# First feed-forward of a two-layer decoder: every expert over every token, or chosen rows scattered into pages by expert

## The chip, the cores and the metric

The kernel runs on one core of one Trainium2 chip, in float32. TensorE does the matmuls (PE; its weight loads are PEld), VectorE is DVE, ScalarE is ACT, GpSimd is POOL, and SyncE (SP) issues DMAs. An engine followed by q (SPq) is that engine's instruction queue. The metric is the device time in microseconds (us).

## The reference

4096 tokens (4 sequences of 1024) of width 256 pass two layers, each with a self attention, a cross attention to 77 context rows, and a feed-forward, all with a residual sum and a layer norm behind them. The change is in the feed-forward of the first layer:

```python
probs = jax.nn.softmax(xf @ router_w + router_b, axis=-1)       # 64 experts
tw, ti = jax.lax.top_k(probs, 8)
tw = tw / jnp.sum(tw, axis=-1, keepdims=True)
def body(acc, p):                                                # one expert, 256 -> 64 -> 256
    W1, B1, W2, B2, e = p
    h = jax.nn.silu(xf @ W1 + B1) @ W2 + B2
    cw = jnp.sum(jnp.where(ti == e, tw, 0.0), axis=-1)           # 0 where e is not chosen
    return (acc + cw[:, None] * h, None)
shared = jnp.sum(jax.vmap(shared_mlp)(sw1, sb1, sw2, sb2), axis=0)   # 2 experts, 256 -> 512 -> 256, all tokens
```

Each token has 8 of 64 experts with a weight other than zero; the reference computes all 64 for all tokens. The router, the choice, the shared experts and the sum over b2 weighted by `cw` belong to it too.

## The kernel before

`decoder` (L1553) runs five phases, one after another, with a barrier and a clearing of semaphores between them (`end_phase`, L1576): attention of layer 0, feed-forward of layer 0, attention of layer 1, feed-forward of layer 1, and the last sum.

**Attention of layer 0** (`attention_phase`, L116) walks the sequence in 8 steps of 128 positions, 4 sequences at once. An order written by hand, `SEQUENCE0` (L91), is the same for every engine: each entry is a stage, how many steps it lags behind, and a part. Iteration n runs a stage with lag a for step n - a; there are 8 iterations plus the largest lag (2). The parts that matter here:

- `ln1` (lag 0, last in the sequence) and `ln2` (lag 2): POOL makes the scale of a layer norm (`norm_scale`, L376: four small operations, L379 to L382), ACT applies it (L486, L496), and POOL adds a bias for the residual (`x1b` L403, `x2s` L411). `x1t`, the first stage of the next iteration, has PE transpose what `ln1` made (L848).
- `wout` (lag 1): PE projects the attention (L965), DVE adds the residual and takes the sums of the norm (L520 to L526), on which POOL's next L379 waits. Its last part stands between `pv` part 3 (DVE: reciprocal and product, L659, L660) and `ln1`.
- `rt`, `top`, `cwt`, `b2` (lag 2): router logits, their softmax and the eight largest (DVE L667 to L688), the weights `cw` transposed and stored to DRAM as `cw1`, and the product with b2 summed into `x2s`, which goes to DRAM as `res1`.
- `ret`, `mx` and `sc` share one PSUM area of four banks ("wide"); the others turn over four banks.

Every engine keeps its instructions in order, so an operation that is late holds back all behind it on that engine. SP prefetches both expert weights, `w1` and `w2` (4096 KB each, L1589 and L1590), into the halves of the tile `big` during this phase.

**Feed-forward of layer 0** (`shared_routed_phase`, L998) goes over 8 tiles of 512 tokens. Each tile has 40 units: 8 of 128 hidden columns of the shared experts, and 32 pairs of routed experts (2 x 64 hidden columns). For each unit PE makes the hidden rows (`hidden`: 2 matmuls over 512 columns), ACT applies bias and silu (L1124), DVE multiplies a routed unit by the token weights of its two experts (L1135, `cw` loaded by broadcasting DMAs, L1063), and PE sums the unit into four output banks (`outward`: 4 matmuls over 256 columns). A float32 matmul appears as two matmul instructions. The tile ends with the residual and a layer norm.

**Attention of layer 1** scatters token rows by expert with indirect DMAs issued by POOL (L423), 8 for each step, 128 rows each, and its feed-forward (`gated_phase`, L1205) reads them back in tiles of 128 rows, transposes them on PE (L1417, L1438), and scatters results (L1309).

## Time and profile before

| | us |
|---|---|
| median of 3 runs (2778.97 to 2783.06) | 2782.24 |
| profiled execution | 2779.99 |
| its span, first to last instruction | 2778.3 |
| attention of layer 0, from 0 to | 532 |
| feed-forward of layer 0, 532 to 1664 | 1132 |
| attention of layer 1, 1664 to 2207 | 543 |
| feed-forward of layer 1, 2207 to 2711 | 504 |
| last sum, 2711 to 2778 | 67 |

Over the span PE is busy 86%, DVE 32%, ACT 23%, POOL 11%; the granted clock of TensorE is 0.92 of full on average. The `windows` view gives, for each stretch, its length, then for PE, PEld, DVE, ACT and POOL the busy time and, in brackets, the number of instructions, and last the granted clock (1.00 is 2.4 GHz, 0.50 is 1.2 GHz), the busy share of the 16 DMA engines and the GB/s that they moved. A line of the timeline gives start and duration in us, engine, source line, operation, what is written and read, and the count of merged instructions; in square brackets stands how long the engine was idle before it, and for whom it waited. A merged line's duration runs to the modelled end of its last instruction; the start of the next line tells better when PE was free.

### The profile page before, as it was taken

What the parts mean: (1) busy time and instruction counts of PE and PEld (TensorE: products, weight loads), DVE (VectorE), ACT (ScalarE), POOL (GpSimd) and SP (SyncE); (2) the same over time, 40 slices, a digit from 0 to 9 for tenths busy, and PEclk for the clock granted to TensorE, in tenths of its full rate; (3) what the DMA queues carried; (4) which work ended last, traced back from release to release, by engine and by line L of the source; (5) the groups of instructions that cost most, each with busy time, mean ns of one, the idle gap of its engine ahead of it and who ended that gap; (6) DMA issues with size and microseconds to landing.
All of it is one profiled execution on the core that took longest, in us unless ns stands there. A gap on an engine that the chain in (4) does not pass through costs nothing. (4 is left out here: it accounts for less than half of the span.)

```text
span 2778.3 us, 47409 instructions
## 1 busy us (share of the span) xinstructions
PE 2379.0 (86%) x18834; PEld 1644.7 (59%) x18835; DVE 895.1 (32%) x2013; ACT 651.8 (23%) x972; POOL 299.1 (11%) x428
## 2 busy tenths in 40 slices
PE   5999898599999999999999975788878259999980
PEld 3777667366666666666666653566656235555550
DVE  4556565212121212121212122445553212222216
ACT  1333223112222212122222111333233012222220
POOL 0111111000000000000000000122321201111111
PEclk9999998699999999999999996789887579999995
DMA  6011100423232323232333224011100321111117
GB/s 200 25 35 37 57 27 27 114 50 77 68 84 61 84 61 84 61 84 63 81 65 80 53 53 168 17 33 38 49 32 25 104 84 42 42 44 44 42 36 242
DMA packets 136392, 185.35 MB, mean 67 GB/s; under 512 B 14379, under 2 KB 94495, under 8 KB 135327
## 3 DMA queue, kind: packets, MB, share of 16 engines
q1 hardware_dynamic: 124319, 156.43, 21.0%
q0 software_dynamic: 7680, 22.16, 2.2%
q10 hardware_dynamic: 4224, 4.19, 0.5%
q8 instruction: 143, 2.34, 0.4%
q14 instruction: 26, 0.21, 0.0%
HBM read 140.65 MB, written 42.11 MB: 66 GB/s over the span
## 5 line engine op out<-in xcount | busy, mean ns | idle before, releaser
L1189 PE MATMUL b_yp<-big,b_h 128*128 128x256 f32 x2048 | 481.2, 379 | 0.0
L1177 PE MATMUL b_hp<-b_xt,big 128*128 128x512 f32 x1024 | 481.2, 592 | 0.0
L1189 PEld LDWEIGHTS b_yp<-big,b_h 128*128 128x128 f32 x2048 | 389.1, 190 | 155.3 <-issue 114.8
L1135 DVE TENSOR_TENSOR b_h<-b_h,b_cw 128x512 f32<-128x512 f32 x256 | 177.3, 693 | 873.9 <-ACT b_h L1124 873.9
L1124 ACT ACTIVATE b_h<-b_hp,b_b 128x512 f32<-128x512 f32 x256 | 176.0, 687 | 705.5 <-PE b_hp L1177 705.5
L1177 PEld LDWEIGHTS b_hp<-b_xt,big 128*128 128x128 f32 x1024 | 194.6, 190 | 135.7 <-issue 122.5
L473 ACT ACTIVATE pt<-wide 77x2048 f32<-77x2048 f32 x64 | 119.9, 1874 | 146.3 <-PE wide L945 146.3
L1429 PE MATMUL d_gp<-big,d_xt 128*128 x288 | 143.9, 622 | 9.8 <-issue 0.6
L1342 DVE TENSOR_TENSOR d_h<-d_gate,d_up 128x512 f32<-128x512 f32 x72 | 49.5, 688 | 298.2 <-PE d_up L1429 298.2
L659 DVE RECIPROCAL rden<-bank 128x256 f32<-128x256 f32 x64 | 112.2, 1754 | 98.2 <-PE bank L957 97.7
L1177 PE MATMUL b_hp<-b_xt,b_sw 128*128 128x512 f32 x256 | 119.7, 601 | 20.1 <-DMA b_sb<-in_L_sb 18.9
L1447 PE MATMUL d_yp<-d_wd,d_ht 128*128 x576 | 136.2, 379 | 0.8 <-ACT d_ht L1326 0.8
L1447 PEld LDWEIGHTS d_yp<-d_wd,d_ht 128*128 128x128 f32 x576 | 109.4, 190 | 46.1 <-issue 35.0
L1429 PE MATMUL d_up<-big,d_xt 128*128 x288 | 135.3, 592 | 0.0
L1189 PEld LDWEIGHTS b_yp<-b_sw,b_h 128*128 128x128 f32 x512 | 97.3, 190 | 40.5 <-issue 30.6
L1189 PE MATMUL b_yp<-b_sw,b_h 128*128 128x256 f32 x512 | 121.0, 379 | 0.0
L1103 POOL TENSOR_TENSOR b_mv<-b_mv,b_eps 128x4 f32<-128x4 f32 x8 | 1.6, 195 | 1092.9 <-DVE b_mv L1156 1092.9
L945 PE MATMUL wide<-peak_t,sel 32*77 32x128 f32 x2048 | 112.6, 289 | 0.1
L652 DVE TENSOR_REDUCE peak<-wide 128x16 f32<-128x1232 f32 x64 | 92.0, 1437 | 33.6 <-PE wide L929 31.4
L965 PE MATMUL bank<-wout,att_t 128*128 128x256 f32 x256 | 74.6, 442 | 28.7 <-DVE att_t L660 28.7
L1429 PEld LDWEIGHTS d_up<-big,d_xt 128*128 128x128 f32 x288 | 54.8, 190 | 69.2 <-issue 69.2
L777 PE MATMUL bank<-xt,wqk 128*128 128x512 f32 x128 | 65.6, 641 | 26.6 <-DVE ones L577 26.6
(237 smaller groups left out, 2817.5 us busy)
## 6 DMA issues: line engine op xcount, KB each, us to landing
b_cw<-cw SPq DMA_DIRECT2D x128, 512.0 KB, 7.5
d_x<-lists SPq DMA_DIRECT2D x72, 130.0 KB
big<-in_L_w SPq DMA_DIRECT2D x2, 4096.0 KB, 20.7
f_y<-results SPq DMA_DIRECT2D x16, 512.0 KB, 7.8
x<-in_x SPq DMA_DIRECT2D x8, 512.0 KB
xt<-in_x_t SPq DMA_DIRECT2D x32, 128.0 KB, 3.2
res_t<-x2t SPq DMA_DIRECT2D x32, 128.0 KB, 1.9
res<-x2s SPq DMA_DIRECT2D x8, 512.0 KB, 3.2
```

The lines of the kernel that those rows point to most:

```text
L473: empties(nc.scalar.activation(pt[0:CTX, p % 2].rearrange("k (j n) -> k j n", j=4), ps[0:CTX], ACT.Exp, scale=score_scale), job)
L652: empties(nc.vector.tensor_reduce(peak[:, p].rearrange("p (j n) -> p j n", j=4)[:, :, 0:4], ps[:, :, 0:4 * CTX].rearrange("p j (n k) -> p ...
L659: step(nc.vector.reciprocal(rden[:, p % 2], ps[:, KC * P:]))
L777: ins = mm(out[:], wqk[:, c, p * P:(p + 1) * P], xt[:, i % 2, c], start=c == 0, stop=c == KC - 1)
L945: ins = mm(out[0:CTX, r, n * P:(n + 1) * P], sel[quarter(r), n], peak_t[quarter(r), toks(p)], start=False, stop=True, skip_group_check=True)
L965: ins = mm(out[:, bb * DM:(bb + 1) * DM], att_t[:, c, toks(2 * p + bb)], wout[:, c], start=c == 0, stop=c == KC - 1)
L1124: nc.scalar.activation(h[:, u % 4], hp[u % 4][:], ACT.Silu, bias=bias).then_inc(h_done, 1)
L1135: nc.vector.tensor_tensor(h[:, u % 4], h[:, u % 4], cw[:, g % 2, p % G], ALU.mult)\
L1177: ins = mm(hp[u % 4][:], w, xt[:, k, c], start=c == 0, stop=c == KC - 1)
L1189: ins = mm(yp[t][:, 0:DM], h[:, u % 4, t * P:(t + 1) * P], sw2[:, u] if u < CH else w2[:, u - CH], start=u == 0, stop=u == UNITS - 1)
L1429: ins = mm(out[k][:], xt[:, k, c], w[:, c, bass.ds(e * H1, H1)], start=c == 0, stop=c == KC - 1)
L1447: ins = mm(yp[:, 0:DM], ht[:, k, c], wd_flat[:, bass.ds(e * (HC * DM) + c * DM, DM)], start=c == 0, stop=c == HC - 1)
```

## The change

Layer 0's feed-forward becomes two phases, and its attention phase gets the work that sorts rows by expert.

1. **Attention of layer 0.** `cw1` and its store go. Two stages without matmuls are new, `put` and `weigh`, both with lag 3, so there is an eleventh iteration; `rank` (lag 2) stands after `b2` and before `pv` part 3. DRAM tensors `lists0` and `results0` have 192 pages of 256 rows of 1 KB, 50.3 MB each. ACT fills `lists0` with zeros ahead of the scatters: ten DMAs of 2 MB at `v` of step 0, two at `v` of each later step. `top` gives the chosen mask and counts as well. `rank` is three float32 matmuls on PE (positions before each token, by a triangular matrix, and totals) and some 20 operations on DVE that turn them into a page and a row for each of a token's 8 choices, kept in the SBUF tile `slots0`. `put` has POOL issue 32 indirect DMAs for each step (4 sequences x 8 choices), each storing 128 rows of 1 KB. `weigh` is three DVE operations over 2048 elements that leave the eight weights in `weights0`. The tile `z2` gets three buffers, so that `wout` waits for the scatters of three steps ago.
2. **`expert_phase`.** `w2` is loaded here, all 64 experts into both halves of the partitions (two DMAs of 4096 KB), no longer in the attention phase. From the page ends DVE works out the expert of each page. Then 96 pairs of pages follow: two loads of 256 KB on SP, 8 transposes (PE), the chosen expert's weights copied by DVE to a small tile at an address that it reads as a value from SBUF, hidden rows and outputs on PE in two halves of the array, moves by ACT and DVE, and two stores of 256 KB issued by POOL.
3. **`combine_phase`.** The 8 tiles of 512 tokens keep only the 8 shared units. POOL gathers each tile's 4 x 8 x 128 rows by 32 indirect DMAs, two tiles ahead of the sums; DVE adds them, weighted, to the tile in 32 operations, and the layer norm follows.

The core of the diff:

```diff
-    ("v", 0, 0), ("ln2", 2, 0), ("x2t", 2, 0), ("x2t", 2, 1),
-    ("ret", 0, 0), ("mt", 1, 0), ("v", 0, 1), ("kt", 0, 0),
+    ("v", 0, 0), ("ln2", 2, 0), ("put", 3, 0), ("x2t", 2, 0), ("x2t", 2, 1),
+    ("ret", 0, 0), ("mt", 1, 0), ("v", 0, 1), ("kt", 0, 0), ("weigh", 3, 0),
...
+    ("rank", 2, 0),
     ("pv", 1, 3), ("wout", 1, 1), ("ln1", 0, 0),
...
+                if stage == "put":
+                    pool.wait_ge(slot_done, i + 1)
+                    pool.wait_ge(blank[i], 16 * len(blanks(i)))
+                    for b in range(NB):
+                        for k in range(K0):
+                            pool.indirect_dma_start(
+                                out=lists, out_offset=bass.IndirectOffsetOnAxis(ap=slots[:, b, i, k:k + 1], axis=0),
+                                in_=z2[i % 3][:, b, :], in_offset=None).then_inc(scattered[i % 3], 16)
...
+                if stage == "v" and p == 0:
+                    act.wait_ge(pool_ready, 3)
+                    for n in blanks(i):
+                        act.dma_start(lists[n * 8 * R0:(n + 1) * 8 * R0, :].rearrange("(p t) n -> p t n", p=P),
+                                      zero[:].unsqueeze(1).broadcast_to([P, 8 * R0 // P, DM])).then_inc(blank[i], 16)
...
+                if stage == "weigh":
+                    dve.wait_ge(cw_done, i + 1)
+                    step(nc.vector.tensor_tensor(same, place[:].unsqueeze(2).broadcast_to([P, NB, K0, E]),
+                                                 slot[:].unsqueeze(3).broadcast_to([P, NB, K0, E]), ALU.is_equal))
+                    step(nc.vector.tensor_tensor(same, same, cw[:].unsqueeze(2).broadcast_to([P, NB, K0, E]), ALU.mult))
+                    step(nc.vector.tensor_reduce(weights[:, :, i, :], same, AX.X, ALU.add))
...
+def expert_phase(nc, sems, d, w1, w_in, lists, page_ends, results):
...
+        @block.sync
+        def _(sp):
...
+            for j in range(PAIRS):
+                if j >= NX:
+                    for h in range(2):
+                        sp.wait_ge(x_full[h], j - NX + 1)
+                for h in range(2):
+                    sp.dma_start(x[:, j % NX, h], rows_of(lists, 2 * j + h)).then_inc(x_in[j % NX], 16)
...
+        @block.gpsimd
+        def _(pool):
...
+                    pool.wait_ge(y_done[h], j + 1)
+                    pool.dma_start(rows_of(results, 2 * j + h), y[:, j % NY, h]).then_inc(sent[j % NY], 16)
...
+        @block.scalar
+        def _(act):
...
+                    turn_out(move, act, 1, j + 1)
+                act.wait_ge(h_full, j + 1)
+                act.wait_ge(staged, 4 * (j + 1))
+                nc.scalar.activation(ht[:, j % 2], hp[j % 2][:, 0:R0], ACT.Silu, bias=w2s[:, j % NW, DM:DM + 1])\
+                    .then_inc(h_done, 1)
+                if j:
+                    rows_out(j - 1)
...
+            def stage(j):
...
+                for h in range(2):
+                    lanes = slice(h * H0, (h + 1) * H0)
+                    e = dve.value_load(plan_i[0:1, j, h:h + 1], min_val=0, max_val=E0 - 1)
+                    nc.vector.tensor_copy(w1s[:, j % NW, h], w1[:, :, bass.ds(e * H0, H0)]).then_inc(staged, 1)
+                    nc.vector.tensor_copy(w2s[lanes, j % NW],
+                                          w2[lanes].rearrange("p e n -> p (e n)")[:, bass.ds(e * (DM + 1), DM + 1)])\
+                        .then_inc(staged, 1)
...
+            def inward(j):
...
+                for c in range(KC):
+                    for h in range(2):
+                        ins = mm(hp[j % 2][h * H0:(h + 1) * H0, 0:R0], w1s[:, j % NW, h, c], xt[:, j % 2, h, c],
+                                 start=c == 0, stop=c == KC - 1)
...
+            def outward(j):
...
+                for t in range(2):
+                    for h in range(2):
+                        ins = mm(yp[h][:, t * DM:(t + 1) * DM], ht[lanes, j % 2, t * P:(t + 1) * P],
+                                 w2s[lanes, j % NW, 0:DM], start=True, stop=True)
...
+            for j in range(PAIRS):
+                if j + 1 < PAIRS:
+                    rows_in(j + 1)
+                inward(j)
+                if j:
+                    outward(j - 1)
...
+def combine_phase(nc, sems, d, src, src_t, results, slots, weights, dst):
...
+            def pick(T):
+                if T >= 2:
+                    pool.wait_ge(summed, (T - 1) * (K0 + 1))
+                for k in range(K0):
+                    for t in range(SUB):
+                        b, i = T // 2, (T % 2) * SUB + t
+                        pool.indirect_dma_start(
+                            out=picked[:, T % 2, t, k, :], out_offset=None, in_=results,
+                            in_offset=bass.IndirectOffsetOnAxis(ap=slots[:, b, i, k:k + 1], axis=0))\
+                            .then_inc(got[T % 2], 16)
...
+                for n in range(K0):
+                    for t in range(SUB):
+                        b, i = T // 2, (T % 2) * SUB + t
+                        ins = nc.vector.scalar_tensor_tensor(out=acc[:, t], in0=picked[:, k, t, n],
+                                                             scalar=weights[:, b, i, n:n + 1], in1=acc[:, t],
+                                                             op0=ALU.mult, op1=ALU.add)
+                    ins.then_inc(summed, 1)
```

## Rows read from the trace of the kernel before

**Rows 1.** The `windows` view by stage: start:end, then busy time and count by engine.

```profile
532.00:1664.00 1132.00, 1104.58 (x3840) 729.91 (x3840) 213.94 (x392) 230.31 (x329) 16.50 (x29) 0.99 0.31 73
...
1969.00:2026.00 57.00, 46.48 (x718) 36.54 (x718) 29.72 (x84) 19.08 (x28) 15.20 (x18) 0.85 0.12 39
```

**Rows 2.** Groups of instructions by line: busy us, mean ns of one.

```profile
L1189 PE MATMUL b_yp<-big,b_h 128*128 128x256 f32 x2048 | 481.2, 379 | 0.0
L1177 PE MATMUL b_hp<-b_xt,big 128*128 128x512 f32 x1024 | 481.2, 592 | 0.0
...
L432 ACT ACTIVATE x1t<-bank 128x512 f32<-128x512 f32 x32 | 18.7, 597 | 93.2 <-PE bank L848 92.4
...
L686 DVE SCALAR_TENSOR_TENSOR rest<-rest,ex 128x256 f32<-128x256 f32 x8 | 3.4, 425 | 0.3
```

**Rows 3.** Timeline of layer 0 attention, one step, then its end: start us, us.

```profile
331.94 0.20 POOL L379 TENSOR_TENSOR rs<-mv,eps 128x4 f32<-128x4 f32 x1 [27.50 <-DVE mv L526]
...
343.16 1.83 PE L848 MATMUL bank<-ident,x 128*128 128x128 f32 x8
...
359.99 2.36 POOL L411 TENSOR_TENSOR x2s<-z,sb 128x1024 f32<-128x1024 f32 x1 [11.62 <-ACT z L496]
...
389.63 0.20 POOL L379 TENSOR_TENSOR rs<-mv,eps 128x4 f32<-128x4 f32 x1 [27.28 <-DVE mv L526]
...
458.65 1.92 PE L848 MATMUL bank<-ident,x 128*128 128x128 f32 x8
...
507.36 0.20 POOL L379 TENSOR_TENSOR rs<-mv,eps 128x4 f32<-128x4 f32 x1 [38.97 <-DVE mv L526]
...
528.15 0.38 SPq L355 DMA_DIRECT2D res<-x2s  x1
```

**Rows 4.** Timeline of POOL, layer 1: first and last of eight indirect DMAs.

```profile
1887.04 1.06 POOL L423 DMA_INDIRECT lists<-rows,slot_u  x1 [25.36 <-DVE slot_u L719]
...
1896.01 0.96 POOL L423 DMA_INDIRECT lists<-rows,slot_u  x1 [0.30 <-issue]
```

**Rows 5.** Timeline of DVE and PE in the step of rows 3.

```profile
340.47 2.89 PE L965 MATMUL bank<-wout,att_t 128*128 128x256 f32 x8 [2.43 <-DVE att_t L660]
...
361.86 2.29 DVE L588 TENSOR_TENSOR prob<-wide,causal 128x2048 f32<-128x2048 f32 x1 [4.95 <-PE wide L800]
...
368.42 0.42 DVE L667 TENSOR_TENSOR lg<-bank,router_b 128x256 f32<-128x256 f32 x1 [4.28 <-PE bank L973]
```

**Rows 6.** Timeline of PE: matmuls on parts of the array, and transposes.

```profile
2010.67 0.66 PE L890 MATMUL bank<-v,tri 128*128 128x65 f32 x4
...
2011.26 0.49 PE L887 MATMUL bank<-state,sig 64*128 64x130 f32 x4
...
2020.06 2.08 PE L911 MATMUL bank<-wo,combt 64*128 64x256 f32 x8
...
2033.19 1.95 PE L857 MATMUL bank<-xt,wlin 128*64 128x256 f32 x16
...
2262.64 0.60 PE L1438 MATMUL d_hp<-d_ident,d_h 128*128 128x128 f32 x4
```

**Rows 7.** The `windows` view: stretches with much DMA, and the one of 2020.06.

```profile
20.00:40.00 20.00, 13.40 (x63) 7.58 (x64) 9.81 (x27) 0.60 (x1) 0.00 (x0) 1.00 1.04 380
...
2020.10:2022.00 1.90, 1.90 (x12) 1.14 (x8) 1.44 (x1) 0.00 (x0) 0.00 (x0) 0.50 0.00 0
...
2720.00:2735.00 15.00, 0.00 (x0) 0.00 (x0) 11.88 (x29) 0.00 (x0) 2.45 (x4) 0.50 0.92 288
...
2735.00:2778.00 43.00, 0.00 (x0) 0.00 (x0) 30.86 (x83) 0.00 (x0) 7.28 (x12) 0.50 0.68 224
```

**Rows 8.** Timeline of SP: issues of DMAs.

```profile
16.16 0.80 SPq L1590 DMA_DIRECT2D big<-in_L_w  x1
...
2236.04 8.01 SPq L1285 DMA_DIRECT2D lists<-d_padding  x8
```

**Rows 9.** Section 6 of the page: KB each, us from issue to landing.

```profile
results<-d_y,d_dest POOLq DMA_INDIRECT x72, 2.4
```

More of the change, by code:

```diff
@@ L27 @@
 CAP = NT + P
+K0 = 8
+R0 = 2 * P
+PAIRS0 = (NT * K0 // R0 + E0) // 2
+ROWS0 = 2 * PAIRS0 * R0
 ROWS1 = NT * K1 // P + E1
@@ L73 @@
 WIDE = ("ret", "mx", "sc")
-MARKS = ("ln1", "ln2", "top")
+MARKS = ("ln1", "ln2", "top", "put", "weigh")
 def steady(sequence):
@@ L190, in attention_phase @@
             kr = sb("kr", [P, NB, DM])
-            prob = sb("prob", [P, 2, 4 * 4 * P])
+            prob = spare[:, 0:4096].rearrange("p (h n) -> p h n", h=2)
+            same = spare[:, 4096:6144].rearrange("p (b k e) -> p b k e", b=NB, k=K0)
+            z2 += [spare[:, n:n + 1024].rearrange("p (b n) -> p b n", b=NB) for n in (6144, 7168)]
+            before = sb("before", [P, P])
+            ones_sq = sb("ones_sq", [P, P])
+            ones_row = sb("ones_row", [P, E])
+            zero = sb("zero", [P, DM])
+            pages_i = sb("pages_i", [P, 2, 2, E], mybir.dt.int32)
+            pages = sb("pages", [P, 2, E])
+            base = sb("base", [P, E])
+            book = sb("book", [P, 4, E])
+            late = sb("late", [P, NB, E])
+            chosen = sb("chosen", [P, NB, E])
+            counts = sb("counts", [P, NB + 1, E])
+            place = sb("place", [P, NB, E])
+            slot = sb("slot", [P, NB, K0])
             ctx_rows = prob[0:CTX, 0, 0:NB * DM].rearrange("k (b n) -> k b n", b=NB)
@@ L259, in attention_phase @@
         sent_rows = sem("sent_rows")
+        mask_done = sem("mask_done")
+        slot_done = sem("slot_done")
+        scattered = [sem(f"scattered{k}") for k in range(3 if first else 1)]
         if first:
@@ L263, in attention_phase @@
             sent_cols = sem("sent_cols")
-            sent_cw = sem("sent_cw")
+            blank = [sem(f"blank{i}") for i in range(STEPS)]
         else:
@@ L388, in _ @@
             nc.gpsimd.memset(peak[:], 0.0).then_inc(pool_ready, 1)
+            if first:
+                nc.gpsimd.memset(zero[:], 0.0).then_inc(pool_ready, 1)
             if not first:
@@ L416, in _ @@
                             .then_inc(copy_done, 1)
-                if stage == "rank":
+                if stage == "put":
[6 more added lines that the diff above has]
+                                in_=z2[i % 3][:, b, :], in_offset=None).then_inc(scattered[i % 3], 16)
+                if stage == "rank" and not first:
                     pool.wait_ge(slot_done, i + 1)
@@ L845, in _ @@
                         b = 2 * p + bb
-                        of = x[:, i % 2, b] if stage != "x2t" else z2[:, b] if first else rows[:, b, 0, 0:DM]
+                        of = x[:, i % 2, b] if stage != "x2t" else z2[i % 3][:, b] if first else rows[:, b, 0, 0:DM]
                         for c in range(KC):
@@ L1085, in _ @@
-            load(0, slice(0, TOK))
+            load(0)
             for a, b in loads:
                 sp.dma_start(a, b).then_inc(consts, 16)
-            weights(0, slice(0, TOK), range(2), first=True)
-            load(1, slice(TOK, 2 * TOK))
-            weights(0, slice(0, TOK), range(2, GROUPS), first=True)
-            with sp.Fori(0, TILES // 2 - 1) as i:
-                for k in range(2):
-                    tile(2 * i + k + 1, k)
-            weights(TILES - 1, slice((TILES - 1) * TOK, TILES * TOK), range(GROUPS))
+            load(1)
@@ L1096, in _ @@
+            for T in range(TILES):
+                sp.wait_ge(out_done, T + 1)
+                sp.dma_start(dst[T * TOK:(T + 1) * TOK, :].rearrange("(t p) n -> p t n", p=P), out[:, T % 2])\
+                    .then_inc(sent[T % 2], 16)
+                if T + 2 < TILES:
+                    sp.wait_ge(y_full, T + 1)
+                    load(T + 2)
+            for k in range(2):
+                sp.wait_ge(sent[k], 16 * TILES // 2)
         @block.gpsimd
         def _(pool):
-            nc.gpsimd.memset(half[:], -0.5)
```

477 lines of the change are left out of this document (313 added, 164 removed).

## The prediction

> **What bounds the kernel now.** I read the `windows` view by stage first. The feed-forward of layer 0 takes 1132 us and PE is busy 1104.6 of them at a granted clock of 0.99 [rows 1]: nothing but TensorE ends there. It does 8 x 40 = 320 units, so a unit costs 1104.6 / 320 = 3.45 us. Four fifths of them (256) are routed pairs, 32 for each tile; DVE and ACT, busy 214 and 230 us, hide behind them. In the groups by line the reader sees that half of this goes into the outward and half into the inward matmuls, 481.2 us each for the routed pairs [rows 2].
>
> Then I read the timeline of the attention step, since the change adds work to all of its engines. A step is 389.63 - 331.94 = 57.7 us from one `ln1` on POOL to the next [rows 3]. PE sets it, except at the end: there PE waits 2.43 us for DVE's last `att_t` [rows 5], so what DVE gets ahead of that product lengthens the step one for one. POOL is nearly idle: its last operation in the step is `x2s` at 359.99, and nothing follows until 389.63 [rows 3].
>
> **The change part by part.** The sum is made against the profiled execution, 2779.99 us (span 2778.3 and 1.7 around it), 2.3 us under the median of the runs.
>
> *Attention, the steps.* `rank` puts about 20 dependent operations on DVE just ahead of `pv` part 3. No row has them. By the neighbours, those over 256 elements take 0.42 us [rows 5] and the small ones about 0.2 (four values take POOL 0.20 [rows 3]): 5 x 0.45 + 12 x 0.25 + four maxima 0.6 + two copies 0.4 = 6.2 us, nearly all on the path. `top` gets one more operation over 256 elements and four short additions, 1.4 us, in a stretch in which DVE has no gap. `weigh` is three operations over 2048 elements of 2.29 us [rows 5], 7 us; between the causal product at 361.86 and the logits at 368.42 DVE idles 4.28 [rows 5], so 2.7 come out late and, wide being held longer, about 1 reaches PE. That makes 8.5 us a step; I take 7.5 for step 2, which has no `weigh`, and 8.5 for five more: 50 us. Bounds: 6 us a step from what follows, and 14 if all of DVE's work counts.
>
> POOL's own cycle must fit too. Consecutive indirect DMAs start (1896.01 - 1887.04) / 7 = 1.28 us apart [rows 4], so 32 take 41.0. From the transposes of `x1t` (343.16) to `x2s` (359.99) are 16.8 us [rows 3]; then 2.4 for `x2s`, 41.0 for `put`, 1.8 for the scale and 2.1 for ACT's norm: 64.2 us, against 57.7 + 8.5 = 66.2 by DVE. So `put` hides behind `rank`; were `rank` free, `put` would still make the step 6.4 us longer. Behind `put` on POOL stands `ln1`, and for it waits the whole next step.
>
> *Attention, the end.* Nothing hides the last scatters. Before, the stage ends 532.0 - 458.65 = 73.4 us after the last `x1t` transposes, and the last `ln2` scale starts 507.36 - 458.65 = 48.7 after them [rows 3]. After: 48.7 + 8.5, then 6.2 for scale, norm and `x2s`, then `put` of steps 6 and 7 one after the other, 82.0, landing 2.4 [rows 9] and barrier 1.4: 149.2. That adds 76 us. With 2 us for two more loads and the memsets at the start, attention costs 2 + 50 + 76 = **+128 us**.
>
> The zero fills are 50.3 MB on ACT's queue, ten of 2 MB at once in step 0. An issue of 4096 KB in 1 KB pieces took SP 0.80 us [rows 8]; ACT idles at `v`, so I cost them at nothing. The trace shows no queue that deep. If ACT had to wait for the queue, up to 21 MB / 288 GB/s [rows 7] = 73 us would be added, once.
>
> *Pages.* PE per pair: 8 transposes at 0.11 us (four take 0.60 with their tail [rows 6]) = 0.9. Inward: 8 instructions of 256 columns in two column halves; 16 such take 1.95 us [rows 6], 8 take 0.94. Outward: 8 instructions in two row halves; 8 took 2.08 us, but at a granted clock of 0.50 [rows 6, 7], so 1.0 at full clock: the halves overlap. Each pair switches the array's form three times. Four 65-column matmuls between two other forms occupy 2011.26 - 2010.67 = 0.59 us where their columns need 0.22 [rows 6]; I take 0.2 per switch. PE: 0.9 + 0.94 + 1.0 + 0.6 = 3.4 us.
>
> The Trainium skill states this switch as a rule, in "TensorEngine Tiling (Array Packing)", Key Properties: changing the tiling mode drains the array. It gives no figure; with no drain the pair would cost PE 2.8 us and the phase 58 us less.
>
> ACT per pair: three moves of 512 columns at 0.60 [rows 2] and a silu of 256, about 0.4 by the same row, 2.2 us. DVE: 0.6 for the turn, four copies of 128 to 257 columns, about 1.1, and two values read into registers. SP's eight issues with such a read took 8.01 us [rows 8], so a read is under 1.0 and DVE under 3.7, in parallel. DMA: 96 pairs move 100.7 MB, 1.05 MB each. At 380 GB/s (large pieces) that is 2.8 us, at 288 (1 KB pieces) 3.6 [rows 7]; these are 2 KB. Three resources thus lie between 3 and 3.7 us. They don't interlock perfectly, so I take the upper end, 3.7, and 96 x 3.7 = 355 us. Ahead of it w2 must land, 8.4 MB at 288 GB/s, 29 us, and x behind it, 4; the last pair and its store add 6, the barrier 2: 396 us.
>
> *Combination.* PE needs 64 x 3.45 = 221 us and POOL 256 x 1.28 = 328: POOL bounds. Seven layer norm scales between gathers, 1.4 each, add 10, the start 1. After the last gather: landing 2.4, 32 sums on DVE of 0.425 [rows 2] = 13.6 and 0.6 of semaphores, norm 4.6, store 2.4, barrier 2: 25. Together 364 us. Whether a gather costs POOL what a scatter does no row shows; from below the columns of the shared units bound the phase (221 + 35), from above see the rivals.
>
> *Sum.* 396 + 364 = 760 for 1132: -372. With +128: 2780 - 244 = **2536 us**.
>
> **The rivals.**
>
> *A, POOL's descriptor work collides with DVE.* During the gathers DVE runs 256 sums whose two inputs both lie in SBUF. If POOL stood still for each, the phase would gain 256 x 0.425 = 109 us [rows 2]: 2645. Against it: the eight scatters of rows 4 kept their pitch while DVE worked, though not with such sums. The Trainium skill, "SBUF — State Buffer", Who interferes with whom, says that a DVE instruction with two SBUF inputs contends with a GpSimd instruction that reads SBUF, and that two-port copies keep GpSimd from writing descriptors; no run so far shows either here.
>
> *B, the pages are paced by data.* In the last 43 us of the kernel, loads and stores mixed reach 224 GB/s [rows 7], though they don't fill the engines there (0.68). At that rate 100.7 MB take 450 us, 95 more: 2631. Or PE loses its clock while waiting: at 0.50 the pair costs 2 x 2.8 + 0.6 = 6.2 us, 240 us more, 2776. Against this speaks layer 1's attention, where PE is busy 46.5 of 57 us and keeps 0.85 [rows 1].
>
> *C, ACT is stopped by the fills:* 40 to 73 us more, 2576 to 2609.
>
> *D, slower than before: an indirect DMA in a long burst costs more than in one of eight.* 512 of them are added in all. The five hidden bursts have 2 us of slack each, so 512 x (p - 1.28) - 10 reaches 244 at p = 1.78 us. At 2.0 us the price is 359 and the time 2895. For it: no burst here is longer than eight; against it: within eight the pitch does not grow (0.96 and 0.30 idle at the last [rows 4]), and each moves 128 KB in 1.28 us, 102 GB/s, far from 288.
>
> *E, better overlap:* pairs at 3.0 us and `rank` cheaper (6 us a step): 2536 - 67 - 15 = 2454.
>
> **How the numbers follow.** Forecast 0.50, A 0.14, B 0.15 (0.02 of it above 2775), C 0.06, D 0.07, E 0.08. The forecast's own range is 2480 to 2610. The range that should hold the time 8 times in 10 runs from 2452 to 2680: it leaves out D, the clockless B and the lower half of E, and some of A and B together. A measurement of this kernel tells 0.2%, 5.6 us, from no change. Faster: all but D, a part of B and their mixtures, 0.90; within: 0.01; slower: 0.09.
>
> **What would show it.** In the trace after: an eleventh iteration of attention with nothing but 32 DMAs on POOL, twice; steps of 66 us, PE waiting some 8 for DVE's `att_t`; ACT's fills issued without a gap. In the pages a pitch of 3.7 us with PE's clock above 0.9 and neither ACT nor DVE without gaps. In the combination POOL back to back at 1.28 us with PE idle a third of the time; a pitch above 1.5 there is A or D, and A if it grows only while DVE sums. The prediction is wrong if pairs take over 5 us, if a burst of 32 slows as it goes, or if ACT stands in step 0.

## The result, and the profile after

The changed kernel takes 2917.1 us (median of 4 runs, 2908.8 to 2921.9) beside 2780.6 for the kernel before on the same chip: ratio 1.049, interval 1.046 to 1.053. The prediction was 2536, faster; the kernel is slower. The profiled execution took 2921.9 us (span 2920.1). By stage, from the `windows` view (columns as in [rows 1]):

```profile
197.00:300.60 103.60, 70.46 (x963) 48.65 (x962) 48.23 (x94) 18.76 (x25) 40.54 (x41) 0.77 0.31 103
300.60:405.00 104.40, 70.34 (x958) 48.51 (x957) 48.35 (x94) 18.67 (x25) 40.81 (x43) 0.75 0.31 102
...
927.90:1304.80 376.90, 302.58 (x2306) 198.87 (x2306) 162.21 (x490) 198.37 (x385) 103.47 (x193) 0.91 0.91 291
1304.80:1804.10 499.30, 261.66 (x768) 161.64 (x768) 143.93 (x384) 43.14 (x65) 255.50 (x275) 0.72 0.32 97
```

The first two rows are steps of attention with a `put`: 104 us where the prediction had 66, and neither PE (70 us busy) nor POOL (41) fills them. The third is the pages, 377 us (predicted 396). The fourth is the combination, 499 (364). Pages and combination together save 256 us of the 1132 of [rows 1]. But attention ends at 927.9 instead of 532.0, 396 us later (predicted 128). Measured on ACT's `ln1` moves, that is 37 at the start, 234 in the seven steps between the first and the last, and 125 behind the last one.

The timeline of one step shows what stands there. POOL's first and last scatter, then PE and ACT (`issue`: the engine waited for nothing that the profile shows; `remote`: for a signal whose sender it does not name):

```profile
441.47 1.04 POOL L447 DMA_INDIRECT lists<-big,slots  x1 [0.16 <-issue]
...
482.81 0.96 POOL L447 DMA_INDIRECT lists<-big,slots  x1 [0.30 <-issue]
...
449.47 0.40 PE L907 MATMUL bank<-big,v 128*32 128x128 f32 x8
...
474.77 0.37 PE L1047 MATMUL bank<-pt,vals 77*32 77x128 f32 x1 [1.72 <-issue]
475.47 0.37 PE L1047 MATMUL bank<-pt,vals 77*32 77x128 f32 x1 [0.33 <-issue]
477.58 0.37 PE L1047 MATMUL bank<-pt,vals 77*32 77x128 f32 x1 [1.74 <-issue]
...
488.07 0.86 PE L1047 MATMUL bank<-pt,vals 77*32 77x128 f32 x10 [0.33 <-issue]
...
488.17 0.60 ACT L468 ACTIVATE ot<-bank 128x512 f32<-128x512 f32 x1 [35.92 <-remote]
```

POOL does nearly what was forecast: 32 scatters start 1.26 us apart, save for two early gaps of 2.3 us, and the last is no slower than in [rows 4]. PE does not. Some 8 us into this burst its groups of eight matmuls fall apart into single ones, started at multiples of 0.7 us, and the idle time ahead of them is put down to `issue`: PE thins out. At 488.07, 4 us after the burst, ten go out at once. PE's clock follows: 0.75 over such a step, 0.50 late in the burst.

The combination shows the same (groups by line, columns as in [rows 2]; third, the idle time and its causes):

```profile
L1374 POOL DMA_INDIRECT b_picked<-results,slots x256 | 245.5, 959 | 77.6 <-issue 77.0 <-POOL b_eps L1380 0.6
L1456 PE MATMUL b_yp<-b_sw,b_h 128*128 128x256 f32 x512 | 139.8, 428 | 155.9 <-issue 81.6 <-ACT b_h L1399 74.3
L1448 PE MATMUL b_hp<-b_xt,b_sw 128*128 128x512 f32 x256 | 134.2, 640 | 69.1 <-issue 41.7 <-DMA b_sb<-in_L_sb 27.3
L1399 ACT ACTIVATE b_h<-b_hp,b_sb 128x512 f32<-128x512 f32 x64 | 43.1, 687 | 438.3 <-remote 215.3 <-PE b_hp L1448 152.1 <-issue 70.9
L1415 DVE SCALAR_TENSOR_TENSOR b_acc<-b_picked,weights,b_acc 128x256 f32<-128x256 f32 x256 | 107.1, 481 | 2.3
```

A gather costs POOL 0.959 us plus 0.30, so 256 of them take 322 us, as forecast. Yet they don't run in one piece. They come in four runs of 64 with gaps of 34 to 38 us: the gathers of tile T + 2 wait until DVE has summed tile T, which waits for PE, and late in each run PE all but stands still (from 1445 to 1508 it is busy 13 of 63 us). What was to overlap comes one after the other.

The start is a matter of its own (timeline of ACT, after, then before):

```profile
1.62 73.86 ACTq L479 DMA_DIRECT2D lists<-zero  x10
75.51 1.28 ACT L468 ACT_TABLE_LOAD   x1 [75.51 <-issue]
76.81 1.09 ACT L468 ACTIVATE v<-bank 128x512 f32<-128x512 f32 x2
```

```profile
37.52 0.60 ACT L432 ACTIVATE v<-bank 128x512 f32<-128x512 f32 x1 [35.38 <-PE bank L782]
```

Ten fills of 2 MB hold ACT for 73.9 us, so its first move of `v` comes 39 us late. The loads are late as well: PE's first matmul starts at 45.31 in place of 26.60. But PE then waits 16.7 us more for ACT's `v`.

### The profile page after: what moved, and what is told of

It is laid out like the page before. It is cut to its first block and busy times, and to the rows that moved or that the text cites. A ratio compares the mean times of both kernels' runs of the same rounds, so it can differ in the third digit from the quotient of the medians.

```text
span 2920.1 us, 47524 instructions
## 1 busy us (share of the span) xinstructions
PE 1946.5 (67%) x18116; PEld 1324.2 (45%) x18117; DVE 1096.4 (38%) x2738; ACT 662.4 (23%) x1093; POOL 908.5 (31%) x1125
## 5 line engine op out<-in xcount | busy, mean ns | idle before, releaser
L1374 POOL DMA_INDIRECT b_picked<-results,slots x256 | 245.5, 959 | 77.6 <-issue 77.0
L1456 PE MATMUL b_yp<-b_sw,b_h 128*128 128x256 f32 x512 | 139.8, 428 | 155.9 <-issue 81.6
L1169 POOL DMA_DIRECT2D results<-e_y x192 | 103.4, 543 | 271.1 <-ACT e_y L1181 268.5
L1448 PE MATMUL b_hp<-b_xt,b_sw 128*128 128x512 f32 x256 | 134.2, 640 | 69.1 <-issue 41.7
L447 POOL DMA_INDIRECT lists<-big,slots x160 | 162.5, 1016 | 48.2 <-issue 47.9
L1047 PE MATMUL bank<-pt,vals 77*32 77x128 f32 x2048 | 105.4, 286 | 96.5 <-issue 96.4
L1399 ACT ACTIVATE b_h<-b_hp,b_sb 128x512 f32<-128x512 f32 x64 | 43.1, 687 | 438.3 <-remote 215.3
L1265 PE MATMUL e_xp<-e_ident,e_x 128*128 128x128 f32 x768 | 106.4, 283 | 42.7 <-DMA e_x<-lists 42.7
L456 POOL DMA_INDIRECT lists<-rows,slot_u x64 | 62.2, 972 | 211.8 <-DVE slot_u L803 194.8
L1408 DVE TENSOR_TENSOR b_acc<-b_yp,b_xr 128x256 f32<-128x256 f32 x32 | 11.3, 418 | 309.5 <-PE b_yp L1456 286.3
L1047 PEld LDWEIGHTS bank<-pt,vals 77*32 77x32 f32 x2048 | 62.9, 112 | 134.9 <-issue 133.7
```

The costliest lines, as they stand in the source:

```text
L447: pool.indirect_dma_start(out=lists, out_offset=bass.IndirectOffsetOnAxis(ap=slots[:, b, i, k:k + 1], axis=0), in_=z2[i % 3][:, b, :], in_ ...
L1047: ins = mm(out[quarter(r), at:at + P], left, pt[0:CTX, p % 2, of:of + P], start=h == 0, stop=h == 1, skip_group_check=True)
L1169: pool.dma_start(rows_of(results, 2 * j + h), y[:, j % NY, h]).then_inc(sent[j % NY], 16)
L1265: ins = tr(xp[h][j % 2][:, (t * KC + c) * P:(t * KC + c + 1) * P], x[:, j % NX, h, t, c * P:(c + 1) * P], ident[:])
L1374: pool.indirect_dma_start(out=picked[:, T % 2, t, k, :], out_offset=None, in_=results, in_offset=bass.IndirectOffsetOnAxis(ap=slots[:, b, ...
L1448: ins = mm(hp[u % 4][:], sw1[:, c, u * P:(u + 1) * P], xt[:, T % 2, c], start=c == 0, stop=c == KC - 1)
```

## The experiments

Each study ran on one chip with the kernel before beside it: e1 to e4, e5 to e8, e9 to e12, e13 to f2 and the last two runs. The five studies ran on five different chips, which turns out to matter. The changed kernel itself did not run again, but kernels with its unpaced bursts did in the first two studies (e1_loops, e4_latefill, e7_fills_bursts8), and their steps took 104 to 106 us as its own did. My theory after the first look (F): a long burst of indirect DMAs keeps the engines' instructions from being fetched.

**e1_loops.** PE's and ACT's code of the combination in loops:

```
-            for T in range(TILES):
+            with pe.Fori(0, TILES // 2) as i:
+                for k in range(2):
+                    T = 2 * i + k
```

> The combination of layer 0 takes 499 us in the changed kernel (1304.8 to 1804.1), 135 more than predicted; PE's records there thin out to single matmuls with idle time put down to issue, and only while POOL issues its gathers. Here PE's and ACT's instructions of the combination stand in loops (PE two tiles an iteration, ACT one) instead of being written out; every matmul, move, gather and wait is the same. Theory F (instruction supply: during a long burst of POOL's indirect DMAs the instruction streams of the other engines are not refilled, and written-out code runs dry): the loop's code is fetched once, PE no longer thins out, POOL's gathers run back to back, the combination takes 365 to 385 us and the whole 2780 to 2805. Rival T (the transfers of the gathers, or their descriptors, slow PE or its semaphores themselves): the same 499 us, 2917 within 10. In between, 420 to 460 us for the combination, would say that only one of the two engines was short of instructions, or only for a part of the time.

2933.2 us against 2785.3; the combination takes 505 us, no less than the 499 of the changed kernel. The packets of the instruction queue in that stage (queue table: packets, MB, share) fell from 7 to 2, the first row from the changed kernel, the second from this one:

```profile
q8 instruction: 7, 0.11, 0.1%
```

```profile
q8 instruction: 2, 0.03, 0.0%
```

So the loops needed next to no new instruction packets, and PE thinned out all the same. That fells F, as far as it means fetching code from DRAM. The Trainium skill, "Runtime: NRT & Kernel Launch", Instruction fetch mechanics, says that instructions are streamed in blocks of 16 KiB by a queue of their own, mostly hidden. The profile of the changed kernel agrees on the blocks (134 packets, 2.20 MB, so 16.4 KB each).

**e2_noput.** No scatters in attention:

```
-                            pool.indirect_dma_start(
-                                out=lists, ...).then_inc(scattered[i % 3], 16)
```

> Left out of the computation: the 256 scatters of the attention stage (the pages stay zero), with the waits on them; rank, weigh and the slots are computed as before, and the fills, pages and gathers stay. Attention ends at 927.9 us in the changed kernel, its steps 3 to 7 take 104.5 each against 66 predicted. If the scatters are what lengthens the steps (theories F and T alike): steps of 64 to 68 us, attention ends at 532 + 37 (late start) + 50 + 10 = 620 to 640, the whole 2615 to 2640. Rival R (rank and weigh on DVE, with their waits, are what lengthens them): steps stay above 90 us, the end falls only by the two bursts after the last step, 82 us, and the whole is about 2835.

2619.3 us, ratio 0.941 (the pages stay zero, so it leaves out a part of the computation). Steps of 65.3 us, attention ends at 627.5. `rank` and `weigh` cost what was forecast (66.2; PE waits 7.0 us for `att_t`, forecast 8). The scatters alone cost 300 us of attention; on this chip, against e1_loops and e4_latefill, 302 and 312.

**e3_plain.** The same bytes as plain DMAs:

```
-                            pool.indirect_dma_start(
+                            at = ((i * NB + b) * K0 + k) * P
+                            pool.dma_start(lists[at:at + P, :], z2[i % 3][:, b, :])
```

> Each of the 256 scatters of the attention stage is replaced by a plain DMA of the same 128 KB from the same tile to a fixed stretch of the pages, issued by POOL at the same place (which leaves the rows of the pages in another order than the computation needs). Same bytes, same count of instructions on POOL, no indices. Theory F1 (what starves the others is that the descriptors of an indirect DMA are written by software): steps near 66 us, attention ends below 700, the whole 2660 to 2720. Rival B (the bytes or the rows of 1 KB, whoever describes them, take the DMA engines from what the other engines need): steps stay within 10 us of 104 or, as plain DMAs are issued faster, are shorter only by the part of the burst that vanishes, 20 us or so: 84, the whole above 2780.

2636.9 us. From its timeline, 32 plain DMAs and the next `ln1` pair:

```profile
323.33 0.20 POOL L402 TENSOR_TENSOR rs<-mv,eps 128x4 f32<-128x4 f32 x1 [13.44 <-DVE mv L564]
...
359.52 17.12 POOL L448 DMA_DIRECT2D lists<-big  x32
...
389.23 0.20 POOL L402 TENSOR_TENSOR rs<-mv,eps 128x4 f32<-128x4 f32 x1 [12.58 <-DVE mv L564]
```

They go out at 0.53 us each, more than twice the bandwidth of the scatters, and the step is 65.9 us. They use the same queue as the scatters (`q0 software_dynamic`, 1536 packets and 4.20 MB between 359 and 389 us), so it is not the queue either. What slows PE is the indirect kind, not the traffic.

**e4_latefill.** The fills behind the constants:

```
+                    if not i:
+                        act.wait_ge(consts, 16 * len(loads))
```

> ACT waits for the constants before it issues the first ten zero fills (20 MB); nothing else is changed. In the changed kernel the fills are issued at 1.5 us, ahead of nearly all loads; the first ln1 scale is on POOL at 91.2 us against 54.5 in the kernel before. If the fills take the DMA engines from the first loads: ln1 near 57 to 62, the whole 30 to 37 us shorter, 2880 to 2888. Rival: the late start comes of the change's other work at the start (two more loads, memsets on DVE and POOL): ln1 stays at 91 and the whole at 2917. A third outcome: the fills then collide with the loads of x for the second step, and only a part, 10 to 20 us, comes back.

2934.2 us; `ln1` at 97.1. The fills now start at 19.6 and hold ACT until 81.9. PE starts at 29.30, nearly as early as before the change, and then waits 38.7 us for ACT's `v`. All three outcomes on record are missed, and the miss names the cause: ACT standing behind its own queue, not the loads.

**e5_spread_cols.** Four bursts of 8 in a step; gathers of 256 B:

```
+                    gate = {0: None, 1: ("mix", i + 3, 1), 2: ("wout", i + 2, 0), 3: ("mx", i + 3, 0)}[part_no]
+                    if gate and gate in plan.place:
+                        filled(pool, gate)
...
-                            out=picked[:, T % 2, t, k, :], ... in_=results,
+                            out=picked[:, T % 2, t, k, 0:64], ... in_=results.rearrange("r (q c) -> (r q) c", q=4),
```

> Two edits, each read from its own stage. (1) Attention: the 32 scatters of a step are issued in four bursts of 8 (one ahead of ln2 of the next step, one after x2s, two later), each held on POOL until PE has filled a named bank, so that 4 to 5 us without a DMA lie between them. (2) Combination: each gather fetches rows of 256 B in place of 1 KB, as many rows; DVE sums four copies of those 64 columns (which changes the computed sums). The looped code of the last study took no instruction packets and PE thinned out all the same, so the supply of instructions is out. Theory S (a long unbroken burst: PE's and ACT's sequencers fall behind only from the 7th or 8th DMA in a row, about 8 us): attention steps of 66 to 72 us, its end near 650; the combination as slow as now, 480 to 500, since the count is the same. Rival V (volume or rate: 102 GB/s through the software queue, in whatever order): steps stay near 100; the combination falls to 370 or less. Rival N (number of rows described per us): steps near 100 and the combination near 499.

2824.3 us. Combination 498 us with a quarter of the bytes: volume is out. Steps 85 to 86 us (the first 92): spreading helps, but not as far as theory S said. In the step from 285.4 to 371.1 PE lost 10.2 us to `issue`, where the changed kernel lost 24.7. In the burst of 8 that starts at 335.77 it thins out after 3 us already and is back at 347.10, 11.3 us after the start. So a long unbroken burst is not needed.

**e6_rows32_pause.** 32 rows per scatter; a pause after each gather:

```
+                ap=slots[0:32, b, i, k:k + 1] ... in_=z2[i % 3][0:32, b, :]
...
+                            rest_made(nc.gpsimd.memset(pad[:], 0.0))
```

> Two edits, each read from its own stage. (1) Attention: each scatter writes 32 rows (the first 32 partitions) in place of 128; 32 scatters in a row as before (three quarters of the pages' rows stay zero). (2) Combination: after each gather POOL fills a spare tile of 1024 columns with zeros and waits for it, about 1.0 us, so that the pitch is 2.3 us in place of 1.26. Theory S (unbroken burst): steps fall only if the burst is over within 8 us: with 32 rows a DMA may take POOL less than 1 us, so between 66 and 90; the combination is POOL's 256 x 2.3 = 590 us and PE never thins out. Rival N (rows described per us): if POOL's time per DMA falls with the rows (0.3 to 0.5 us) steps stay long only for that time; in the combination PE thins out by half as much. What tells them apart is PE's time for a tile while gathers run: 28 us (its columns) or over 40.

3023.4 us. Steps 105 us with a quarter of the rows: rows are out too. The last scatter and PE's recovery:

```profile
485.55 1.65 PE L1047 MATMUL bank<-pt,vals 77*32 77x128 f32 x25 [0.33 <-issue]
```

The burst began at 439.01 at a pitch of 1.17 us and PE was back 46.5 us later; in the changed kernel the pitch is 1.26 and it took 46.6 (441.47 to 488.07). In e1_loops, 64 gathers begin at 1421.15 and ACT is back at 1511.24, 90.1 us later. With e5's 11.3 us for 8, that is 1.41 to 1.46 us for each DMA, though POOL's pitch is less: it looks like a backlog behind POOL, worked off at that rate. In the combination, with a pitch of 2.2 us, PE's outward matmuls lost nothing to `issue` (it took 604 us, set by POOL):

```profile
L1463 PE MATMUL b_yp<-b_sw,b_h 128*128 128x256 f32 x512 | 118.3, 379 | 0.0
```

**e7_fills_bursts8.** One fill with each move of `v` and `kt`; a pause after every 8th gather:

```
-                if stage == "v" and p == 0:
+                if stage in ("v", "kt"):
+                    n = 4 * i + (2 if stage == "kt" else 0) + p
```

> Two edits, each read from its own stage. (1) Start: the 24 zero fills of 2 MB are issued one at a time with each move of v and kt on ACT, four a step, in place of ten at once in step 0 and two a step after. ACT was held 73.9 us by the ten issues (1.62 to 75.5) and PE waited 16.7 for v. Theory C (ACT stopped by the fills): ln1 of step 0 on POOL at 55 to 62 us in place of 91, 30 to 36 us off the whole. Rival: bandwidth, the fills delay the loads wherever they are: ln1 above 80. (2) Combination: after every 8th gather five zero fills of a spare tile on POOL, about 4.7 us. Theory S (unbroken burst): PE never thins out, idle put down to issue falls from 80 us to under 20; POOL's own time is then 32 x (10.1 + 4.7) = 474 us and bounds, the combination ends within 480 to 500. Rival V or N: PE thins out as before and the combination takes 560 or more, since the pauses come on top.

2924.6 us. `ln1` at 62.96 in place of 91.2: 28 us back. The combination took 520 (expected 480 to 500), set by POOL, PE at 379 ns a matmul and 0.0 idle as above.

**e8_putpause_bursts4.** A pause of 512 columns after each scatter, one after every 4th gather:

> Two edits, each read from its own stage. (1) Attention: after each scatter POOL fills a spare tile of 512 columns (0.5 us) and waits for it: pitch about 1.9 us, 32 in 60 us. (2) Combination: after every 4th gather three zero fills of 1024 columns, about 2.8 us. Theory S (a pause ends the burst, however short): steps are set by POOL's own cycle, 60 + 24 = 84 us in place of 104, PE without gaps put down to issue; combination bound by POOL at 64 x (5.0 + 2.8) = 500 us with PE undisturbed. Rival V or N (the mean rate counts): PE is slowed for less of the time but longer, steps 104 or more; in the combination PE thins out as before.

2871.7 us. Steps 83.0 to 84.5 us (expected 84; the first 96), PE's matmuls almost without gaps (1.5 us put down to `issue` in the step from 391.6 to 475.1). The combination took 551, again set by POOL, where 500 stood. S and a backlog fit these pauses alike; a backlog says how long they must be, which the next study varies.

**e9 to e12**, all with the fills of e7, the pause varied in width: `pad = sb("pad", [P, W])`, W = 4, 160, 320, and 768 after every fourth.

> All four kernels of this call issue the zero fills one by one (as the last study did, which brought ln1 of step 0 from 91 to 63 us) and put a pause on POOL after each indirect DMA of the attention and of the combination: a zero fill of a spare tile and a wait for it. Here the tile has 4 columns: by the rows so far a DMA takes 0.96, the fill 0.10 and the wait 0.28, pitch 1.34 us against 1.26. In bursts without a pause PE recovers 1.4 us times the number of DMAs after the burst's start (32: 46.6 us at a pitch of 1.26, 46.5 at 1.17; 64: 89.6), so theory B (a backlog: something that all engines share takes 1.40 to 1.46 us for each indirect DMA and PE and ACT stand behind it once POOL is ahead): at 1.34 the backlog still grows, by 0.1 a DMA; PE thins out late in a burst, steps 80 to 100 us, combination 430 to 490, the whole 2750 to 2870. Rival W (POOL's wait between two DMAs is what frees the others, however short): steps 24 + 32 x 1.34 = 67 us, combination 256 x 1.34 + 36 = 379, the whole about 2600.

> Spare tile of 160 columns, pitch 1.47 us. Theory B (service of 1.40 to 1.46 us for each DMA): just slow enough, PE never thins out; steps 24 + 32 x 1.47 = 71 us in place of 104.6, combination 256 x 1.47 + 36 = 412 in place of 499; attention ends at 928 - 28 - 5 x 33.6 + 13 = 745, the whole 2640 to 2670. Rival W gives the same here. Rival D (duty: POOL must be idle for a third of the time or more, as in the pauses tried so far): PE still thins out, steps above 85, combination above 450, the whole above 2760.

> Spare tile of 320 columns, pitch 1.60 us. Theory B and W: PE undisturbed, POOL bounds: steps 24 + 32 x 1.60 = 75 us, combination 256 x 1.60 + 36 = 446, the whole 50 to 70 us above the kernel with 160 columns. Rival D: faster than with 160 columns.

> The pause comes after every fourth indirect DMA alone, 768 columns: within four the pitch is 1.26, the mean over the burst is (4 x 1.26 + 0.73) / 4 = 1.44 us. Theory B (the mean rate counts): nearly as with 160 columns at each DMA, steps 70 to 74, combination 405 to 420, the whole 2630 to 2670. Rival W (each DMA must be waited behind): PE thins out within the fours but recovers in each pause, steps 80 or more, the whole above 2720.

2855.4, 2811.7, 2764.7 and 2810.9 us, beside 2786.5 for the kernel before. The combination goes as theory B says: 444 us at a pitch of 1.36, and with nothing lost on PE 428 at 1.49, 457 at 1.63, 409 at fours (mean 1.45; so the mean counts, and W falls). Attention does not: steps of 103 to 105, 97 to 102, 81 to 89 and 101 to 104 us, where B had 80 to 100, 71, 75 and 70 to 74. Rival D, a duty, has the better of it there (steps above 85 at 160 columns, and 320 faster than 160), but not in the combination, where it wanted over 450 us in place of 428. The `windows` view of ten microseconds late in a burst (from 22 us after its start, in e11 from 31) counts what PE issued; one row each of the changed kernel, e9, e10, e11 and e8:

```profile
463.47:473.47 10.00, 3.48 (x9) 1.14 (x9) 0.00 (x0) 0.00 (x0) 7.57 (x9) 0.50 0.29 105
```

```profile
442.34:452.34 10.00, 5.30 (x22) 1.36 (x20) 0.00 (x0) 0.00 (x0) 7.77 (x16) 0.50 0.70 235
```

```profile
436.75:446.75 10.00, 9.50 (x66) 4.25 (x61) 1.96 (x2) 0.00 (x0) 8.05 (x14) 0.50 0.67 226
```

```profile
417.40:427.40 10.00, 9.20 (x159) 6.95 (x151) 4.42 (x8) 0.83 (x1) 8.33 (x13) 0.50 0.23 82
```

```profile
420.56:430.56 10.00, 8.67 (x241) 7.40 (x231) 8.50 (x23) 4.14 (x3) 8.38 (x11) 1.00 0.22 78
```

Matmuls and weight loads together: 1.8 per us at a pitch of 1.26, 4.2 at 1.36, 12.7 at 1.49, 31 at 1.63, 47 at 1.83. The last two are no measure of a limit. PE lost almost nothing to `issue` in e8, and in e11 its granted clock is 0.50; the changed kernel, right behind its burst and at the same clock, issues 31 per us (85 in 2.70 us) with nothing in the way:

```profile
488.00:490.70 2.70, 2.63 (x43) 2.28 (x42) 0.00 (x0) 0.60 (x1) 0.00 (x0) 0.50 0.02 6
```

In e11 only 3.4 us of a step went to `issue`, and its steps end with POOL's burst. The combination needs 24 in 3.45 us, 7 per us; attention's small matmuls run at 47 and more where nothing holds them. That fits that 1.49 is enough for the one and not for the other. It looks like a supply of instructions, taken up for some 1.4 us by each indirect DMA; theory I below is this reading, and it is a fit (the changed kernel and e8 ran on other chips than e9 to e11).

**e13_quarters, e14_quarters_slow.** Four times the instructions for the same columns in the combination:

```
+                for part in range(4):
+                    at = slice(part * TOK // 4, (part + 1) * TOK // 4)
```

> The kernel with a pause of 160 columns after each indirect DMA (pitch 1.49), with one more edit in the combination: each matmul is issued as four of a quarter of its columns, the same columns in four times the instructions, 96 in place of 24 (matmuls and weight loads) for a unit of 3.45 us. There the attention's bursts left PE 12.7 instructions per us at this pitch. Theory I (a limit on instructions): a unit takes 96 / 12.7 = 7.6 us, a tile 60 us and more in place of 50, PE and not POOL sets the end, combination 490 to 560 us in place of 428. Rival X (a limit on PE's time or columns): 428 to 440 us, POOL still bounds.

> As e13_quarters, with a pause of 512 columns in the combination, pitch 1.83 us; control for what quarter matmuls cost by themselves. Theory I: 47 instructions per us are left, a unit in quarters needs 28, so PE runs freely, 28 to 35 us a tile, and POOL bounds: 256 x 1.83 + 36 = 505 us, with PE's idle time put down to data and not to issue. If quarters themselves are slow (over 6 us a unit), the combination takes over 520 and PE's records show it without gaps; then e13_quarters says nothing.

2645.5 and 2724.1 us; 430 and 497 us in the combination: POOL bounds in both. But the study can't decide: attention, which in e13 is e10's to the instruction, took 73 to 76 us a step here and not 99. The limit was not there.

**f1_paced, f2_paced384.** Pauses and places as theory I asks:

```
-    ("v", 0, 0), ("ln2", 2, 0), ("put", 3, 0), ("x2t", 2, 0)
+    ("mx", 1, 0), ("put", 4, 2), ... ("ln2", 2, 0), ("put", 3, 0), ("put", 3, 1), ("x2t", 2, 0)
...
+                    if first and i >= 2:
+                        put(i + 2, i - 2, 3)
```

> What theory I asks for. Fills one by one. Combination: a pause of 768 columns after every fourth gather (409 us in e12_fours). Attention: a pause of 512 columns after each scatter (pitch 1.83), and the 32 scatters of a step where POOL stands idle: 16 after x2s, 8 between ln1 and ln2 of the next step, 8 between its ln2 scale and x2s; none paced once PE has no work beside them. Each step then has 35 us ahead of its x2s and 16 x 1.83 = 29 us behind, 64, less than PE's and DVE's own 65.2 (the steps without scatters). Steps 66 to 70 us, attention ends at 690 to 720 in place of 928, the whole 2590 to 2640. Rival: the two bursts ahead of x2s delay ln2 and the products that need x2, steps of 75 or more, the whole 2640 to 2700.

> As f1_paced with a pause of 384 columns in the attention, pitch 1.69. Theory I: 35 to 37 instructions per us left, PE in the steps needs more in places: bursts are 8 % shorter and the stretches in them slower. If what delays a step in f1_paced is POOL's order, this is up to 20 us faster; if it is PE's supply, up to 20 us slower.

2649.6 and 2652.9 us against 2779.3, ratios 0.953 (0.950 to 0.955) and 0.954 (0.952 to 0.957), so the width of the pause made no difference. Steps of 70 to 86 us in f1: the rival came true. The bursts ahead of `x2s` delay it and with it `z`, for which PE waits 7.5 us, in e10_again 2.1 (waits of PE in one step of f1):

```profile
PE bank L952 <- ACT z L549: 7.5, 1, 7.5
PE bank L1069 <- DVE att_t L718: 6.7, 1, 6.7
```

The new places brought nothing: attention ends at 755 us in f1 and at 738 in e13_quarters on the same chip, with e10's plain pauses. What f1 has ahead is the combination, 410 against 430.

**e10_again, e13_again.** The two kernels once more, on one chip:

> The kernel with a pause of 160 columns after each indirect DMA, word for word, on the same chip as e13_again. If the chip made the difference: attention steps as in e13_again, both 99 or both 73 (the whole near 2810, or near 2645). If the program did: 99 here and 73 there.

> The kernel with quarter matmuls in the combination, word for word, beside e10_again. The program makes the difference if the attention stage, in which the two don't differ by an instruction, ends near 738 us here and near 891 there. Should this one now take 99 us a step as well, the chip or the run decides, and in the combination the quarters (7.6 us a unit by theory I) get their test after all: 490 to 560 us against 428.

2655.3 and 2659.5 us against 2778.0, ratio 0.957 (0.954 to 0.959) both; steps of 72 to 75 us both (the first 87). So the program did not make the difference. The same kernel took 2811.7 us in one study and 2655.3 in another, while the kernel before stood at 2786.5 and 2778.0. What changed is the chip, or something that holds for a whole study on it: each chip was visited once. PE in e10_again, in a burst with the same pitch:

```profile
380.00:390.00 10.00, 7.52 (x259) 6.63 (x259) 9.27 (x32) 2.22 (x2) 8.05 (x15) 1.00 0.55 185
```

52 instructions per us, against 12.7. Unpaced bursts were slow each time that they ran (the changed kernel, e1 and e4, e7); they were not run on the chips of the last two studies. So how much of the gain from 2917 to 2655 is the pauses' and how much the chip's is not settled. On one chip, 1.63 against 1.36 us of pitch gave 91 us (2855.4 to 2764.7), and pauses of 512 columns in the attention 82 us of its end (832 us in e8 against 914 in e7, which had the early start).

## Why the prediction was wrong

Term by term, against the changed kernel's trace:

- *Attention, the steps: predicted +50, measured +234.* This is the step that failed: "So `put` hides behind `rank`". POOL's time was right (41.0 predicted, 42.3 here); what was missing is that POOL's burst all but stops PE and ACT. The work it was laid beside could not run. Without scatters seven steps cost +36 (e2_noput), so `rank` and `weigh` were, if anything, overpriced.
- *Combination: predicted 364, measured 499.* The same step, in the words "POOL bounds", which leave PE's 221 us hidden behind POOL. The price of a gather was right. But the last gather starts at 1735 and not near 1643, for POOL waits for PE through DVE, and 69 us follow it where 25 stood. The pauses bring 409 (e12_fours).
- *The end: +76 against +125.* From ACT's last `ln1` to POOL's last `ln2` scale it took 57.9 us before, 65.9 without scatters, as forecast, and 105.0 here: 39 of the 49 missed are the burst of step 5 beside PE's work, the failed step again. From there to the end it took 102.2, where 92.0 stood; the two unhidden bursts themselves took 84 us where 82 stood.
- *Start: +2 against +37.* "I cost them at nothing" took one issue of 0.80 us for ten [rows 8]. Rival C had the mechanism and nearly the size (40 to 73 us), with a chance of 0.06; e7_fills_bursts8 gave 28 us back.
- *Pages: 396 against 377.* The small miss is luck. A pair took 3.2 us between the first and the last transposes (979.1 to 1285.8), where 3.7 stood, 48 us less; the loads ahead took 51 us for 33, and the end 19 for 8. In the steady part PE is busy 295.9 of 306.8 us at a clock of 0.99 and hardly waits, and never for a load, so PE paces it. Its three groups take 1.03, 1.02 and 1.06 us, 3.1 in all, where the prediction's rows make 2.8 without a switch, so the three switches cost some 0.3 us together and not 0.6. The DMA engines are close behind, 0.93 busy at 320 GB/s. The 288 GB/s taken for rows of 1 KB is the mean of a window with a gap in it; from 30 to 40 us the kernel before moves such rows at 349. Rival B's 224 is a mean with gaps as well.
- Sum of the misses: 184 + 135 + 49 + 35 - 19 = 384, and 2536 + 384 = 2920.

Rival D, the one rival priced above the kernel before (chance 0.07), had the place (512 indirect DMAs) but not the mechanism: it priced a longer pitch on POOL, and the pitch never grew. Of the signs named for being wrong, ACT standing in step 0 came true; none named PE thinning out beside a burst. Rival A looked for a collision with DVE; DVE's sums took 0.481 us, the same with dense gathers as with pauses of 1 us between them (0.482 in e6_rows32_pause).

Shown by the runs: the indirect kind of DMA does it, not bytes, rows, bandwidth, the software queue or instruction packets; a lower rate of issue frees PE. Fitted and not shown apart: that a shared supply of instructions is what runs short, and the 1.4 us as its unit. Its own test (e13, e14) ran where the limit did not show. Open: why PE was nearly free at a pitch of 1.49 on two of the chips.

## What to carry to other kernels

A run of indirect DMAs on one engine is not background work, and bursts of eight can cost too (10 us a step in e5): before laying it beside small matmuls, run the two together and read PE's idle time put down to `issue`. If PE thins out, pace the DMAs (here one every 1.5 to 1.8 us), and measure on more than one chip. Big fills go out one by one, from an engine that has nothing urgent behind them.

## What the runs showed of the hardware

- Within a burst of indirect DMAs at 1.26 us, PE thinned out after 8 us (in e5, with bursts of eight, after 3) and was down to 2 instructions per us after 22, and ACT stood idle 36 us ahead of its next move in attention and 23 to 33 in the combination; plain DMAs of the same bytes on the same queue, twice as fast, did nothing of the kind.
- Neither 32 rows in place of 128 (pitch 1.17 in place of 1.26) nor 256 B in place of 1 KB per row changed it.
- PE or ACT recovered 1.41 to 1.46 us times the number of DMAs after the burst's start (8, 32 and 64 of them).
- With pauses on POOL between them PE was held less: on one chip 4.2 instructions per us at a pitch of 1.36 us and 12.7 at 1.49, and 3.4 us lost in a step at 1.63.
- The same kernel differed by 5.9% between two chips, each measured once, on which the kernel before differed by 0.3%.
- Ten issues of 2 MB in rows of 1 KB held ACT 73.9 us. In e7 one at 1.62 took 0.63 us, two at 43.49 and 46.52 took 0.53 and 0.52, and the next, at 47.11, 7.10.
- Three changes between matmuls on the whole array, on column halves and on row halves cost a pair of pages some 0.3 us together (3.1 us measured, 2.8 by the rows of the kernel before).
